# New orders of work, operands placed by 64 bytes and matmuls of zeros, in a transformer block on one core

## What is computed

```
x = x + layernorm(attention(layernorm(x)))
x = x + layernorm(relu(layernorm(x) @ W1 + b1) @ W2 + b2)
```

## Time and profile before

| | us |
|---|---|
| median of 3 runs | 2043.78 (2039.88 to 2043.97) |
| profiled execution, its own time | 2041.29 |
| its span, first to last instruction | 2039.5 |
| TensorE busy | 1926.4 (94%) |
| VectorE busy | 1511.4 (74%) |
| ScalarE busy | 1406.0 (69%) |
| GpSimd busy | 741.6 (36%) |

### The profile page before, as it was taken

How to read it: one execution, slowest core, us unless ns; L and a number is a source line. 1 busy time by engine, 2 the same in 40 slices (tenths; PEclk the granted TensorE clock), 3 DMA queues, 4 the chain that set the end, 5 groups by cost and what they waited for, 6 DMA issues and landing times. The chain is left out here.

```text
span 2039.5 us, 71012 instructions
## 1 busy us (share of the span) xinstructions
PE 1926.4 (94%) x27904; PEld 1575.7 (77%) x27904; DVE 1511.4 (74%) x2913; ACT 1406.0 (69%) x2343; POOL 741.6 (36%) x910
## 2 busy tenths in 40 slices
PE   5789999999999999999999999999999999999985
PEld 3458888777878877888777788787788887778775
DVE  4687777787777778778777777777777777876731
ACT  1457767777776777776677777677777677776763
POOL 3113333334333334433343433333433333343343
PEclk7799999999999999999999999999999999999997
DMA  5333434433333433333343333343334344333200
GB/s 144 74 70 80 89 77 86 85 76 82 81 81 79 93 79 80 79 81 81 82 85 80 79 77 81 80 94 78 77 77 86 76 87 85 78 81 69 56 28 17
DMA packets 132815, 160.60 MB, mean 79 GB/s; under 512 B 29408, under 2 KB 82400, under 8 KB 132576
## 3 DMA queue, kind: packets, MB, share of 16 engines
q1 hardware_dynamic: 130544, 154.13, 35.7%
q10 hardware_dynamic: 2032, 2.69, 0.4%
HBM read 38.21 MB, written 17.83 MB: 27 GB/s over the span
## 5 line engine op out<-in xcount | busy, mean ns | idle before, releaser
L817 DVE TENSOR_REDUCE max_bias<-p_pair 128x4 f32<-128x1024 f32 (+1 forms) x640 | 772.8, 1222 | 262.0 <-PE p_pair L571 139.8
L742 ACT ACTIVATE probs<-p_pair 128x1024 f32<-128x1024 f32 x640 | 634.8, 1026 | 208.4 <-PE p_pair L568 127.6
L964 POOL TENSOR_TENSOR h_lo<-h_f,h_hi 128x512 fp32r<-128x512 f32 x256 | 329.7, 1288 | 507.5 <-ACT h_hi L774 507.5
L571 PE MATMUL p_pair<-stack 49*128 49x256 f32 (+1 forms) x3072 | 319.6, 306 | 39.5 <-DVE max_bias L817 22.7
L774 ACT ACTIVATE h_f<-p_pair,b_s 128x256 f32<-128x256 f32 x512 | 248.8, 486 | 133.1 <-PE p_pair L598 133.1
L571 PEld LDWEIGHTS p_pair<-stack 49*128 49x128 f32 (+1 forms) x3072 | 226.9, 188 | 126.7 <-DVE max_bias L817 59.8
L598 PE MATMUL p_pair<-w_hi,h_hi 64*128 64x256 f32 x2048 | 309.4, 279 | 5.0 <-ACT h_hi L774 2.5
L598 PE MATMUL p_pair<-x_hi,w_hi 64*128 64x256 f32 (+1 forms) x2560 | 302.1, 306 | 9.6 <-DVE x_lo L827 5.2
L598 PE MATMUL p_pair<-w_hi,h_lo 64*128 64x256 f32 x2048 | 305.7, 275 | 0.0
L598 PE MATMUL p_pair<-w_lo,h_hi 64*128 64x256 f32 x2048 | 305.5, 275 | 0.0
L598 PE MATMUL p_pair<-x_hi,w_lo 64*128 64x256 f32 (+1 forms) x2560 | 297.7, 302 | 0.0
(11 more groups left out here) (81 smaller groups left out, 2792.9 us busy)
## 6 DMA issues: line engine op xcount, KB each, us to landing
stack<-qk SPq DMA_DIRECT2D x1536, 64.0 KB, 2.3
xr<-x SPq DMA_DIRECT2D x32, 512.0 KB, 4.2
out<-yf SPq DMA_DIRECT2D x64, 256.0 KB, 2.2
xa<-x SPq DMA_DIRECT2D x31, 512.0 KB, 3.8
shift_rows<-max_t SPq DMA_DIRECT2D x128, 8.0 KB, 1.4
stack<-shift_rows SPq DMA_DIRECT2D x128, 8.0 KB
probs<-w_qkv_t SPq DMA_DIRECT2D x2, 384.0 KB, 5.5
ya<-w ACTq DMA_DIRECT2D x1, 512.0 KB, 8.2
```

Of the source, the lines that this page charges most:

```text
L571: last = nc.tensor.matmul(dst[:, j, col:col + HALF].rearrange("p (a n) -> p a n", a=2), stack[r, stationary, at, kb * P:(kb + 1) * P], two ...
L742: nc.scalar.activation(probs[:, prob_slot(quad, c), :, :], banks("scores", n)[:, :, :], ACT.Exp, scale=SCALE).then_inc(exp_done, 1)
L817: nc.vector.tensor_reduce(dst, src, axis=AX.X, op=ALU.max, negate=True).then_inc(red_done, 1)
L964: nc.gpsimd.tensor_tensor(h_parts[1][:, m:m + 2, :], h_f[:, n % 2, :, :], h_parts[0][:, m:m + 2, :].bitcast(F32), ALU.subtract).then_inc(h ...
```

## The change

**Orders.** All lists of the three tables are new, and so are the pairs of banks of the jobs. The jobs, and the work in each, are the same. For most jobs the new place is one or a few entries from the old.

**Places.** The `sb` lines are in another order, and each row of `stack` is 16 values (64 bytes) longer, so that its second half begins at an odd multiple of 64 bytes. By the same count `w_hi`, `w_lo`, `ident`, the first half of `stack`, `qk` and `probs` are now even; the second half of `stack`, `xa`, `x1_hi`, `x1_lo`, `o_t`, `o_n`, `o2`, `xr`, `x2`, `h`, `max_bias` and `values` are odd. So where both operands of a matmul of `qk`, `v`, `scores_max`, `scores`, `x1`, `o_t` and `max_t` began at even places, one now begins at an even and one at an odd place. `op`, `f1`, `f2`, `x2` and `o2` had that already.

**Zeros.** In batch 0 TensorE multiplies a 128 x 128 float32 tensor of zeros by itself: 16 times ahead of `x1`, 4 times ahead of `qk` 0 and `qk` 2, and 5 times ahead of each `scores_max` whose number is 0 or 1 modulo 5 (eight of them), 64 in all. They stand behind the wait for the job's pair of banks and ahead of the job's other waits, and write into that pair.

```diff
+IDLE = {"x1": 16, "qk": 4, "scores_max": 5}
...
-        stack = sb("stack", [P, 2, PAIRS, L], F32R)
-
-        max_bias = sb("max_bias", [P, 2, 4 * KB + D])
...
+        stacks = sb("stacks", [P, 2, PAIRS * L + 16], F32R)
+        stack = stacks[:, :, 0:PAIRS * L].rearrange("p a (n l) -> p a n l", l=L)
+
+        qk = sb("qk", [P, 2, 4, L], F32R)
+
+        probs = sb("probs", [P, CH + 2, 2, L])
+        x1_old = sb("x1_old", [P, KB, D])
+        h_f = sb("h_f", [P, 2, 2, HALF])
+        yf = sb("yf", [P, KB, D])
+        b2_s = sb("b2_s", [P, D])
+        ya = sb("ya", [P, KB, D])
         bqk_s, b1_s = sb("bqk_s", [P, 4]), sb("b1_s", [P, KF])
...
+        max_bias = sb("max_bias", [P, 2, 8 * KB + D])
...
+        zeros = sb("zeros", [P, P])
...
+            pe.wait_ge(zeros_set, 1)
+
+            def keep_busy(dst, times):
+
+                for _ in range(times):
+                    nc.tensor.matmul(dst[:, 0, 0:P], zeros[:, :], zeros[:, :], start=True, stop=True)
+
             def job(what, n, b):
                 dst = banks(what, n)
...
+                if isinstance(b, int) and b == 0:
+                    keep_busy(dst, IDLE.get(what, 0) if opens(what, n) and (what != "scores_max" or n % CH < 2) else 0)
...
+            nc.vector.memset(zeros[:, :], 0.0).then_inc(zeros_set, 1)
```

Of the tables the lines of `ORDER["PE"]` around `x1` stand for the rest:

```diff
-        ("scores_max", 13, -1, 2), ("scores_max", 14, -1, 1), ("op", 1, -2, 3), ("x1", 0, 0, 2),
-        ("scores", 3, -1, 1), ("f2", 0, -3, 0), ("max_t", 2, -1, 3), ("scores", 4, -1, 1),
...
+        ("op", 0, -2, 3), ("scores_max", 13, -1, 2), ("x1", 0, 0, 0), ("op", 1, -2, 3), ("scores", 3, -1, 2),
+        ("f2", 0, -3, 1), ("scores", 4, -1, 2), ("qk", 0, 0, 0), ("scores_max", 14, -1, 3),
```

More of the change, by code:

```diff
@@ L54 @@
+        ("exp", 7, -1), ("exp", 8, -1), ("exp", 9, -1), ("relu", 4, -3), ("relu", 5, -3), ("relu", 6, -3),
+        ("qk_hi", 2, 0), ("qk_hi", 3, 0),
     ],
     "DVE": [
+        ("normal_o", 1, -3), ("ln2_mean", 1, -4), ("f2_out", 1, -5), ("reduce", 3, -2), ("reduce", 4, -2),
+        ("lnf_stats", 1, -5), ("ln1_apply", 1, -1), ("lnf_mean", 1, -5), ("ln2_apply", 0, -4),
         ("copy_max", 0, -2), ("reduce", 5, -2), ("reduce", 6, -2), ("lnf_shift", 1, -5), ("reduce", 7, -2),
-        ("reduce", 8, -2), ("normal_o", 2, -3), ("ln2_apply", 1, -4), ("reduce", 9, -2), ("normal_o", 3, -3),
@@ L68 @@
-        ("lnf_mean", 1, -4), ("ln1_apply", 1, 0), ("ln2_mean", 1, -3),
+        ("normal_o", 2, -3), ("reduce", 8, -2), ("ln2_apply", 1, -4), ("reduce", 9, -2), ("normal_o", 3, -3),
+        ("x2_lo", 0, -4), ("reduce", 10, -2), ("v_out", 0, -2), ("o2_lo", 0, -3), ("reduce", 11, -2),
+        ("copy_max", 1, -2), ("reduce", 12, -2), ("reduce", 13, -2), ("x1_lo", 0, -1), ("op_out", 0, -3),
+        ("lny_stats", 0, -3), ("lny_stats", 1, -3), ("lny_mean", 0, -3), ("reduce", 14, -2), ("reduce", 15, -2),
@@ new lines @@
+        ("ln1_stats", 1, 2), ("reduce", 3, 1), ("reduce", 4, 1), ("reduce", 5, 1), ("copy_max", 0, 1),
+        ("reduce", 6, 1), ("normal_o", 2, 0), ("reduce", 7, 1), ("reduce", 8, 1), ("reduce", 9, 1),
+        ("ln1_mean", 1, 2), ("ln1_apply", 0, 2), ("ln1_apply", 1, 2), ("normal_o", 3, 0), ("v_out", 0, 1),
+        ("reduce", 10, 1), ("o2_lo", 0, 0), ("reduce", 11, 1), ("copy_max", 1, 1), ("reduce", 12, 1),
+        ("reduce", 13, 1), ("x1_lo", 0, 2), ("op_out", 0, 0), ("lny_stats", 0, 0), ("reduce", 14, 1),
@@ new lines @@
+        ("ln2_mean", 0, 0), ("normal_o", 1, 1), ("ln1_mean", 0, 3), ("reduce", 4, 2), ("ln2_apply", 0, 0),
+        ("reduce", 5, 2), ("ln1_mean", 1, 3), ("ln2_mean", 1, 0), ("copy_max", 0, 2), ("reduce", 6, 2),
+        ("normal_o", 2, 1), ("reduce", 7, 2), ("reduce", 8, 2), ("reduce", 9, 2), ("ln2_apply", 1, 0),
+        ("normal_o", 3, 1), ("x2_lo", 0, 0), ("ln1_apply", 0, 3), ("reduce", 10, 2), ("v_out", 0, 2),
+        ("o2_lo", 0, 1), ("ln1_apply", 1, 3), ("reduce", 11, 2), ("copy_max", 1, 2), ("reduce", 12, 2),
@@ new lines @@
+        ("lnf_mean", 1, -5), ("reduce", 4, -2), ("lnf_shift", 1, -5), ("ln2_apply", 0, -4), ("copy_max", 0, -2),
+        ("reduce", 5, -2), ("reduce", 6, -2), ("reduce", 7, -2), ("normal_o", 2, -3), ("reduce", 8, -2),
+        ("ln2_apply", 1, -4), ("reduce", 9, -2), ("normal_o", 3, -3), ("x2_lo", 0, -4), ("reduce", 10, -2),
+        ("ln1_apply", 1, -1), ("v_out", 0, -2), ("o2_lo", 0, -3), ("reduce", 11, -2), ("copy_max", 1, -2),
+        ("reduce", 12, -2), ("reduce", 13, -2), ("x1_lo", 0, -1), ("op_out", 0, -3), ("lny_stats", 0, -3),
```

440 lines of the change are left out of this document (207 added, 233 removed), and 18 rows, old and new, of tables (LAST, ORDER).

## The result

The changed kernel takes 2073.19 us (median of 3 runs, 2071.49 to 2074.27) against 2043.78 us before: ratio 1.0149, 95% interval 1.0126 to 1.0172, slower by 30 us. The forecast was 2007 us, with 2041 as the upper end of the range: wrong in its sign.

A forecast was written before the change was run, and what follows sets the result against it. TensorE, busy 94% of the span, was taken as the bound, with gains from its waits. About -1.0 us a turn over 28 turns (-28), start -4 and end -3 sum to -35: 2007 us, range 1978 to 2041.

The forecast's parts named there:

- Around `x1`: Steady state: `scores` 3 takes an earlier-freed pair of banks, so its wait behind `x1` goes, -0.53 us a turn.
- Around `pv` 1: Steady state: 0.5 us of wait for `relu` 7 moves from `scores` 10 to `scores_max` 2, net 0.
- Small late arrivals: First stretch: five other jobs, 0.45 us together too long, lose half of it, -0.2 us a turn (0 to -0.45).
- Middle stretch: TensorE from the end of `f2` 3 to `v` 0, 11.01 us: no change, between -0.3 and +0.62 us.
- the slower rival: VectorE's middle stretch gets longer, `scores` 18 waits for `copy_max` 0, +0.62 us a turn: 2057 us, chance 0.14.
- Last stretch: Last of three parts of a turn, 14.72 us with 0.10 idle: no change, between -0.3 and +0.3 us.
- Places: Mixed even and odd operand places save up to 5 ns on 88 matmul pairs: -0.25 us a turn (0 to 0.44).
- The rival that it does nothing: The new placement has no effect, 7 us less gain: 2014 us, chance 0.15.
- Start: First batches: clock gains of 3.1 and 3, zeros' price +6.4, new orders -4: sum -4 us, between -14 and +8.
- perhaps a quarter: Start, until 62.9 us: a raised clock brings a quarter of the 11 us full speed would save, -3 us.
- End: Last batch: earlier `op` brings the last `x2` 4.6 us sooner, `f2` 0 costs +2.4: -3 us (-9 to +2).
- Only the ends count: Rival: another job waits what `scores` 3 stops waiting, turn stays 59.9 us, ends give 7: 2036 us, chance 0.10.

The follow-up runs named there:

- short_relu_changed: The changed orders without zeros, with further order edits, and steady-state `relu` 0 to 3 writing `h_f` for 32 of 256 columns only: 2042.32 us, ratio 0.9986.
- vector_apart: Changed kernel without zeros, with `ln1_apply` 0 moved behind `reduce` 2 and `ln2_stats` 1 in VectorE's steady-state list: 2057.18 us, ratio 1.0050 to before.
- change_no_zeros: The whole change without the matmuls of zeros: 2066.53 us, ratio 1.0091 to the kernel before.
- places_alone: The kernel before with the new places alone, old orders and no zeros: 2043.60 us, ratio 0.9982.
- tail_again: Changed kernel without zeros, with the tail of the kernel before put back but `o2` between `f1` 2 and `f1` 1: 2063.68 us, ratio 1.0103.

## Why the prediction was wrong

*Around `x1`: -0.53 us a turn.* The wait went, and the gain didn't come. The step that failed reads "Next in line would be `qk` 0 ...; `f2` 0 lies ahead of it and covers them": I asked what follows `f2` 0, and not what `f2` 0 itself waits for. It needs `relu` 3, as `short_relu_changed` shows. With the stretch from `f1` 1 to `f2` 0 at 6.74 us and the floor at 6.42, 0.32 was to be had; and since `scores_max` 14 left the stretch, 0.24 of that was only its work done elsewhere. What was won is 0.09 us.

*The collision: missing from the sum, +0.4 to +0.5.* It is the largest term of what came out, and the forecast had nothing for it. It could have been seen ahead: the new lists of GpSimd and VectorE, laid side by side by time, put `ln1_apply` 0 beside `h_lo` 7. I moved VectorE's instructions about with the durations of the earlier trace rows, as if they kept them in other company. The Trainium skill, "SBUF — State Buffer", section "Who interferes with whom", which the prediction cites for TensorE, says in the same place that GpSimd and VectorE share a pair of ports, held for a whole instruction by whoever comes first, that `tensor_scalar` can take it and that `tensor_reduce` does not. The traces agree: `ln1_apply` takes 0.41 us alone and 1.40 beside GpSimd's 1.31, while VectorE's reductions take 1.21 to 1.23 us whatever GpSimd does. GpSimd, which came first, lost next to nothing (`h_lo` takes 1.30 us in the median, 1.29 in the kernel before).

*Around `pv` 1: 0.* `scores_max` 2 did inherit a little of the wait (0.34 us instead of 0.24). `max_t` 3 fell from 0.55 to 0.19 us, so this place gained some 0.2 us.

*Small late arrivals: -0.2.* They went from some jobs and came to others: the stretch from `f2` 0 to the end of `f2` 3 holds 1.42 us above the jobs' own lengths before, and 1.41 in `vector_apart`. The term was 0.

*Middle stretch: 0, bounds -0.3 to +0.62.* 11.17 us by the medians against 11.01, +0.16, inside the bounds. `copy_max` 0 ended 5.76 us behind `f2` 3; I had put the point of decision at 5.6. So the slower rival was right in its sign of this term, and small.

*Last stretch: 0.* +0.05 above the jobs' own lengths.

*Places: -0.25.* About 0.1 us in either orders, no more than two traces of one turn differ by. `v` did not come to 114 ns a pair (median spacing inside a job: 118.5 before, 118.2 in `change_no_zeros`, 118.0 in `places_alone`), so the difference of `v` and `op` in the earlier trace rows did not rest on the places. `f1` did get faster, from 118 to about 115 ns in `places_alone`, and in every kernel with the new places, though by my count of the places nothing had changed for it: what the placement acts on I can't say. The rival that it does nothing was right as far as times go.

Summed by the medians: -0.09 + 0.48 (the collision, with the arrivals) + 0.16 + 0.05 = 0.6 us a turn, where -1.0 was forecast.

*Start: -4, came out +14.* The -3.1 for `qk` 0 and 1 at full speed did not come. `qk` 0 takes 2.99 us with the zeros and without; over it the row of clocks says 0.50 in the change and 1.00 before, so in the first 20 us that row doesn't tell the pace. Over `qk` 1 it says 0.98 and the matmuls are faster than before, but `qk` 2 waits for VectorE behind them, and `scores_max` 0 starts at 27.86 us instead of 26.76. From 28.8 to 62.9 us the clock was higher (0.78, against 0.60 in `change_no_zeros` and 0.50 before), and "perhaps a quarter" of full speed's saving was given to a stretch in which VectorE was busy for 23.91 of 34.1 us; nothing of it came. The zeros cost 3.4 us up to the second `x1` and 5.2 up to the fifth (240.2 against 235.0), less than my 6.4, but with nothing to set against them. The larger part, 8.7 us, is in the orders, where the forecast's 4 us, "should take out some waits as in a turn", had no row behind them: 5.3 us are `h_lo` 3 in GpSimd's first list and the clock behind that stall. The 3.4 us that are left were not looked into; from the second `x1` to the fourth the new orders take 117.3 us against 111.9.

*End: -3, came out +10.* The chain `op_out`, norm, `x1_add`, norm was taken for the bound because it filled the idle time of the earlier trace rows. The binding one ran beside it, from `f2` 3 of the batch before through `final_add` 1, which reads `x1_old`. In the change `op` stands ahead of six more jobs of that batch, and the binding chain came 5.8 us later while the other came 10 us sooner. With the old tail put back that `f2` 3 was still 4.4 us later than before (`tail_again`), so the orders ahead of the tail have a share that was not looked into. The +2.4 us for the last batch's `f2` 0 were of the right kind: from the last `x2` to the end it is 48.7 us against 44.3, and 47.4 to 50.7 in all kernels with the new tail against 44.3 to 46.9 in all with the old.

Two readings ahead of the sum were off as well, and changed nothing in it: fourteen `scores` and `scores_max` jobs stand in the middle stretch, not fifteen, and the shortest length of each job in the kernel before adds up to 54.4 us a turn, not 55.3.

None of the rivals was this one. "Only the ends count" said what happens at `x1`, but not at what price elsewhere.

## What to carry to other kernels

When an instruction is moved, its duration has to be read again with what the other engines do at its new time; for VectorE and GpSimd, lay both lists side by side. When a wait is taken away, ask for every later job up to the next fixed point what it waits for by itself, and measure the distance to the latest of those: that distance, and not the wait, is the gain. At the end of a program two chains can end at the same instruction, and the one that is easier to see need not be the one that binds, so follow the last waiting instruction back through the write-after-read as well, and through lists of other engines in which a job of the next batch can stand ahead of one that is needed now.
